# A fused attention layer on one core: values of two steps in one group, maxima of two heads in row halves, queries projected two slots ahead

## The reference

```python
qkv = einsum('bchw,oc->bohw', x, w_qkv);  q, k, v = split(qkv, 3)
q = q.reshape(b, 8, 64, n) * 64 ** -0.5          # k, v alike, unscaled
attn = softmax(einsum('bhdi,bhdj->bhij', q, k), axis=-1)
out = einsum('bhij,bhdj->bhid', attn, v)
y = einsum('bchw,oc->bohw', out, w_out) + b_out
y = y * rsqrt(mean(y * y, axis=1) + 64 ** -0.5) * rms_scale
return y + x
```

## Time and profile before

| | before |
|---|---|
| median of 3 runs | 4428.12 us (4426.63 to 4432.22) |
| the profiled execution's span | 4424.5 us |
| PE busy | 4317.8 us, 98% |
| DVE busy | 2982.6 us, 67% |
| POOL busy | 2722.1 us, 62% |
| ACT busy | 1984.7 us, 45% |

### The profile page before, as it was taken

One profiled execution on the slowest core, in us unless ns is written; L12 is line 12 of the kernel. 1 busy time (PEld: TensorE's weight loads), 2 busy tenths in 40 slices (PEclk: granted clock), 3 DMA queues, 4 the chain that ended last, 5 costly groups with the idle time before them and its releaser, 6 DMA issues.

```text
span 4424.5 us, 61545 instructions
## 1 busy us (share of the span) xinstructions
PE 4317.8 (98%) x18752; PEld 2583.7 (58%) x18752; DVE 2982.6 (67%) x2506; ACT 1984.7 (45%) x3265; POOL 2722.1 (62%) x2092
## 2 busy tenths in 40 slices
PE   7999999999999999999999999999999999999996
PEld 5556565565655656555565655656556565565653
DVE  5567666676766667676666666676667766676665
ACT  3445444444444444444444444544445444454443
POOL 5566656665566665666666565665656755666565
PEclk9999999999999999999999999999999999999998
DMA  3111111111111101111021110211101111111100
GB/s 134 39 48 48 39 42 55 49 48 39 58 39 49 60 27 63 39 53 58 20 77 36 42 58 21 76 39 39 58 31 66 39 39 58 49 48 39 45 32 29
DMA packets 71359, 213.19 MB, mean 48 GB/s; under 512 B 8152, under 2 KB 8280, under 8 KB 58208
## 3 DMA queue, kind: packets, MB, share of 16 engines
q1 hardware_dynamic: 71008, 208.80, 13.4%
HBM read 168.92 MB, written 39.85 MB: 47 GB/s over the span
## 4 chain that ended last, share of the span: by engine, by line
PE 94%; DVE 3%; issue 2%; ACT 1%; POOL 0%; DMA 0%; POOLq 0%; SPq 0%; ACTq 0%; DVEq 0%
PE pv L539 22%; PE aux L424 16%; PE aux L477 12%; PE score L524 12%; PE score L526 10%; PE aux L460 8%; PE aux L505 8%; PE aux L491 2%; DVE maxima L749 2%; PE aux L484 1%; PE aux L514 1%; DVE x_lo L266 0%; ACT v_sb L623 0%; ACT x_hi L669 0%; DVE o_norm L794 0%
## 5 line engine op out<-in xcount | busy, mean ns | idle before, releaser
L884 POOL TENSOR_TENSOR prob_sum<-prob_sum,probs 128x512 f32<-128x512 f32 x1536 | 2004.4, 1333 | 538.0 <-ACT probs L593 537.4
L593 ACT ACTIVATE probs<-score 128x512 f32<-128x512 f32 x2048 | 1112.2, 595 | 1339.8 <-PE score L526 1264.4
L749 DVE TENSOR_REDUCE maxima<-aux 128x1 f32<-128x1024 f32 x1024 | 1236.9, 1218 | 300.1 <-PE aux L477 284.8
L539 PE MATMUL pv<-probs,v_sb 128*64 128x512 f32 x4096 | 1104.4, 618 | 0.0
L880 POOL TENSOR_TENSOR prob_sum<-probs 128x512 f32<-128x512 f32 x256 | 323.3, 1284 | 1062.8 <-ACT probs L593 1062.8
L524 PE MATMUL score<-q_hl,k_hh 128*128 128x512 f32 x2048 | 857.4, 419 | 24.1 <-ACT v_sb L623 22.8
L526 PE MATMUL score<-q_hm,k_l 72*128 72x512 f32 x2048 | 813.1, 397 | 0.0
L477 PE MATMUL aux<-k_hh,q_hl 128*128 128x512 f32 x2048 | 709.4, 428 | 22.3 <-DVE maxima L749 21.4
L424 PE MATMUL aux<-x_hi,w_ring 128*128 128x512 f32 x2048 | 646.1, 397 | 17.3 <-POOL x_lo L266 17.3
L477 PEld LDWEIGHTS aux<-k_hh,q_hl 128*128 128x128 f32 x2048 | 343.8, 189 | 489.0 <-issue 313.2
L524 PEld LDWEIGHTS score<-q_hl,k_hh 128*128 128x128 f32 x2048 | 386.5, 189 | 350.3 <-issue 205.5
(11 more groups left out here) (58 smaller groups left out, 3694.3 us busy)
## 6 DMA issues: line engine op xcount, KB each, us to landing
w_ring<-w_split SPq DMA_DIRECT2D x93, 1024.0 KB, 4.8
x_stage<-x SPq DMA_DIRECT2D x128, 256.0 KB, 4.4
resid<-x SPq DMA_DIRECT2D x128, 256.0 KB, 5.7
out<-resid SPq DMA_DIRECT2D x128, 256.0 KB, 2.0
w_split<-w_ring SPq DMA_DIRECT2D x3, 1024.0 KB, 12.1
w_split<-y_sb SPq DMA_DIRECT2D x3, 1024.0 KB, 3.8
y_sb<-wqkv SPq DMA_DIRECT2D x4, 512.0 KB, 8.3
probs<-wqkv SPq DMA_DIRECT2D x2, 512.0 KB, 7.0
```

Of the source, the lines that this page charges most:

```text
L539: pe.matmul(pv[half][e * D:(e + 1) * D, :], v_sb[:, pair // 2, j, (pair % 2) * P + e * D:(pair % 2) * P + (e + 1) * D], probs[:, j % 4, e, ...
L593: act.activation(probs[:, j % 4, e, :], score[e][:], ACT.Exp, scale=SOFT).then_inc(prob_ready, 1)
L749: dve.tensor_reduce(maxima[:, n:n + 1], aux[at][:], AX_X, ALU.max).then_inc(aux_free[at], 1)
L884: pool.tensor_tensor(prob_sum[:, e, :], prob_sum[:, e, :], probs[:, j % 4, e, :], ALU.add).then_inc(prob_added, 1)
```

## The change

A slot still has 8 steps, now laid out on 16 places of another order:

- The values of two steps are one group: places 1, 5, 9 and 13 hold the values of steps 2g-2 and 2g-1 (g = t // 4; at place 1 the last slot's steps 6 and 7). L stands at place 5, ahead of the values.
- Behind each value group stand the maxima of one query tile for both heads (`maxima_of_tile`). They use the queries' and keys' high parts alone, 64 rows each: head 0 in rows 0 to 63, head 1 in rows 64 to 127. For this, head 1's queries are kept with the high part in the upper rows. Each tile takes all four banks: head 0 banks 0 and 1, head 1 banks 2 and 3.
- The other items stand at places 3, 7, 11 and 15. K is two items of one bank, the values' projection four. T stands in the middle of Q at place 15, and is now one pass of a 128 x 128 product in the split form's operand type.
- Q projects for the slot after the next (`SLOT_QUERIES = 2`).
- `aux` is one tensor of four banks with their own counters.
- L's sums are copied to SBUF by ACT, and DVE inverts them in two halves at places 5 and 6; `normalise` moves to place 8, O0 and O1 to place 11.
- DVE splits five of x's eight parts in slot 6, POOL three. SP's weight loads wait for other items.

```diff
-SUMS_AT = (1, 1, 1, 1, 1, 1, 1, 1)
-VALUES_AT = (3, 3)
-MAXIMA_AT = [(4, 5, 6, 7, 8, 9, 10, 11)] * SLOTS
-OUTPUT_AT = [(12, 14)] * SLOTS
-NORMALISE_AT = 5
+SLOTS, STEPS, BLOCKS = 8, 8, 4
+PLACES = 4 * BLOCKS
+SLOT_QUERIES = 2
+SQUARE_AT = (2, 4, 6, 8)
+NORMALISE_AT = 8
+INVERT_AT = ((0, 12), (1, 12))
+ROOT_AT = ((1, 0), (2, 0))
+SCALE_AT = ((1, 2), (2, 2))
+REPEAT_AT = 10
+SPLIT_AT = (0, 1, 2, 4, 5, 6, 8, 9)
+SPLIT_BY_GPSIMD = (1, 3, 5)
...
+    if t % 4 == 1:
+        if t == 5 and preceding:
+            out.append(("L", 3))
+        if following:
+            out += [(f"M{t // 4}0", 0), (f"M{t // 4}1", 2)]
+    if t in (3, 7):
+        if slot in (0, 2, 4):
+            out.append((f"K{t // 4}", 0))
+        elif slot in (1, 3):
+            out.append((f"V{slot - 1 + t // 4}", 0))
+        elif slot == 7 and following:
+            out.append((f"V{t // 4}", 0))
+    if t == 11:
+        if preceding:
+            out += [("O0", 0), ("O1", 2)]
+        if slot == 6 and projected:
+            out.append(("K0", 0))
+        if slot == 7 and following:
+            out.append(("V2", 0))
+        if slot in (0, 1) and not first:
+            out.append(("R", 0))
+    if t == 15:
+        if following:
+            out.append(("T", 2))
+        if projected:
+            out.append(("Q", 0))
+        if slot == 6 and projected:
+            out.append(("K1", 1))
+        if slot == 7 and following:
+            out.append(("V3", 1))
...
+            def maxima_of_tile(body, slot, it):
+                nslot = (slot + 1) % SLOTS
+                npair, nhalf = divmod(nslot, 2)
+                ks = [claim(body, slot, f"M{it}{e}", two=True) for e in range(2)]
+                for h in range(2):
+                    for e in range(2):
+                        rows = slice(e * D, (e + 1) * D)
+                        last = pe.matmul(bank(ks[e] + h), q_hl[rows, nhalf, e, it * P:(it + 1) * P],
+                                         k_hh[rows, npair % 2, e, h * HALF:(h + 1) * HALF],
+                                         start=True, stop=True)
+                        if h == 1:
+                            last.then_inc(aux_full[ks[e]], 1)
...
-                    for t in range(HALF_STEPS):
-                        j = t // 2
+                    pe.wait_ge(q_repeated, 2 * (body.b * SLOTS + slot + 1))
+                    for t in range(PLACES):
+                        g = t // 4
+                        names = [name for name, _ in items_at(slot, t, body.first, body.last)]
                         if t % 2 == 0:
-                            scores(body, slot, j)
-                        elif j > 0:
-                            values(body, slot, j - 1, False)
+                            scores(body, slot, t // 2)
+                        elif t % 4 == 1:
+                            if "L" in names:
+                                item(body, slot, "L")
+                            for j in (2 * g - 2, 2 * g - 1):
+                                if g > 0:
+                                    values(body, slot, j, False)
+                                elif slot > 0:
+                                    values(body, slot - 1, STEPS + j, False)
+                                elif not body.first:
+                                    values(body, SLOTS - 1, STEPS + j, True)
+                            if f"M{g}0" in names:
+                                maxima_of_tile(body, slot, g)
+                        elif "Q" in names:
+                            item(body, slot, "Q", range(0, 2))
+                            item(body, slot, "T")
+                            item(body, slot, "Q", range(2, KT))
+                            for name in names:
+                                if name not in ("Q", "T"):
+                                    item(body, slot, name)
...
+                elif name == "L":
+                    done = body.b * SLOTS + slot
+                    k = body.full(act, slot, name)
+                    if not (body.first and slot == 1):
+                        act.wait_ge(onorm_ready, done - 1)
+                    act.activation(inv_sum[:], bank(k), ACT.Copy).then_inc(aux_free[k], 1)
...
+            def invert_sums(body, slot, part):
+                if part == 0:
+                    body.consumed(dve, slot, "L")
+                cols = slice(part * HALF // 2, (part + 1) * HALF // 2)
+                dve.reciprocal(inv_sum[:, cols], inv_sum[:, cols]).then_inc(inv_ready, 1)
...
+                        if t in (5, 6) and preceding:
+                            invert_sums(body, slot, t - 5)
+                        for name, _ in items_at(slot, t, body.first, body.last):
                             item(body, slot, name)
...
-                        if t == NORMALISE_AT and not (body.first and slot == 0):
+                        if t == NORMALISE_AT and preceding:
                             normalise(body, slot)
-                        if t == NORMALISE_AT + 2 and slot not in LOW_BY_GPSIMD:
+                        if t == NORMALISE_AT + 1 and slot not in LOW_BY_GPSIMD:
                             split_output_low(dve, body.b * SLOTS + slot)
```

More of the change, by code:

```diff
@@ L60, in items_at @@
     preceding = not (first and slot == 0)
     out = []
-    if t == 0 and following:
-        out.append("Q")
-    if t == SUMS_AT[slot] and preceding:
-        out.append("L")
-    if following:
-        out += [f"M{i}" for i, at in enumerate(MAXIMA_AT[slot]) if t == at]
-        if slot == 7:
-            out += {2: ["K"], 3: ["V0"], 15: ["V1"]}.get(t, [])
-    if slot in (1, 2) and t == VALUES_AT[slot - 1]:
-        out.append(f"V{slot - 1}")
-    if slot in (0, 1) and t == MEAN_AT[slot] and not first:
-        out.append("R")
@@ L99, in body_keys @@
-def body_keys(first, last):
-    return [(s, n) for s in range(SLOTS) for t in range(HALF_STEPS) for n in items_at(s, t, first, last)]
+    if t % 4 == 1:
[10 more added lines that the diff above has]
+            out.append((f"V{t // 4}", 0))
@@ L103, in attention_kernel, with body_items @@
+def body_items(first, last):
+    return [(s, n, k) for s in range(SLOTS) for t in range(PLACES) for n, k in items_at(s, t, first, last)]
 def attention_kernel(nc, x, wqkv, wout, bias, scale, consts, out):
@@ L486, in item @@
+                    last.then_inc(aux_full[k], 1)
+                elif name == "T":
+                    k = claim(body, slot, name)
+                    body.consumed(pe, slot, "M30")
+                    body.consumed(pe, slot, "M31")
+                    if body.plan is pro:
+                        pe.wait_ge(mask_set, 2)
+                    pe.matmul(bank(k)[:, 0:P], maxima[:], neg_ident[:],
+                              start=True, stop=True).then_inc(aux_full[k], 1)
                 elif name == "L":
@@ L694, in _ @@
             start = Body(pro, -1, True, True)
+            for slot, name, _ in PRO_ITEMS:
+                item(start, slot, name)
+                if (slot, name) == (6, "Q"):
+                    repeat_queries(start, 7)
             act.wait_ge(const_loaded, 64)
-            for name in PRO_ITEMS:
-                item(start, 7, name)
             act.wait_ge(w_set, 3)
@@ L741, in item @@
[L741 to L745 removed]
+                        ins = dve.tensor_tensor(k_l1[0:D, kp, e, cols], bank(k)[rows[e], :],
+                                                k_hh[rows[e], kp, e, cols].bitcast(F32), ALU.subtract)
+                    ins.then_inc(aux_free[k], 1)
+                    for e in range(2):
+                        dve.tensor_copy(k_hh[rows[1 - e], kp, e, cols], k_hh[rows[e], kp, e, cols].bitcast(F32))
@@ L820, in one @@
                 for slot in range(SLOTS):
-                    for t in range(HALF_STEPS):
+                    preceding = not (body.first and slot == 0)
+                    for t in range(PLACES):
                         if (slot, t) in SCALE_AT and not body.first:
@@ L849, in _ @@
             dve.tensor_copy(tile_mask[:], raw_mask).then_inc(mask_set, 1)
-            dve.wait_ge(mask_set, 1)
+            dve.tensor_copy(neg_ident[:], raw_ident).then_inc(mask_set, 1)
+            dve.wait_ge(mask_set, 2)
             start = Body(pro, -1, True, True)
-            for name in PRO_ITEMS:
-                item(start, 7, name)
+            for slot, name, _ in PRO_ITEMS:
+                item(start, slot, name)
             run_bodies(dve, one)
             end = Body(epi, B, False, True)
-            item(end, 0, "L")
+            for part in range(2):
+                invert_sums(end, 0, part)
             normalise(end, 0)
```

405 lines of the change are left out of this document (180 added, 225 removed).

## The result

The changed kernel takes 5013.17 us (median of 4 runs, 5006.92 to 5017.71) against 4427.38 before: 1.132 times the time, 95% interval 1.1304 to 1.1336. I had forecast 4484 and a range up to 4625. The sign was right, the size wrong by 529 us: the change cost ten times what I had forecast.

What follows compares the result with a forecast made beforehand. Bound by PE's instruction stream; PE saves 20.8 us a batch (268.2 to 247.4), waits add 27.3; with slot schedules, 275.2 against 271.9, plus prologue and epilogue: 4484 us, 1.3% slower. Own range 4425 to 4545; eight in ten 4290 to 4625.

Steps and rivals of the forecast that it cites:

- The value group: Values of two steps in one group on PE: 2.01 us where 2.45 stood; four groups save 1.75 a slot.
- the maxima in pairs: Maxima groups on PE, two pairs in row halves: 0.76 us each; four groups 3.0 a slot for 3.7.
- T: T in one pass on PE, at place 15: saves 0.15 us a slot.
- Rival 2: Maxima groups: row halves don't run side by side, 7.9 us a batch more, 4610 us; chance 0.12.
- rival 3: Maxima groups: weights of a row half wait for that half's matmul, 0.11 us a group, 4540 us; chance 0.05.
- the waits in the batch: PE's added waits on DVE, the output projection's chain and late reductions: 15.0 + 8.7 + 2.4 + 1.2 = 27.3 us a batch.
- `o_lo` from DVE in slots 2 and 6: Before O0 at place 11, behind group 2's reductions in program order: 2.5 us more in slot 2, 4.0 in slot 6.
- Rival 1: Places 7 and 11: DVE's chain isn't late, only 0.43 us bank waits remain, 4306 us; chance 0.30 in full, 0.12 by half.
- Batch 247.4 + 27.3: One batch: 247.4 us if nothing waited plus 27.3 of waits, 274.7 against 271.9 before.
- PE busy near 90%: Sign in the trace after: PE busy near 90% of the span, against 98% before, would bear the forecast out.
- two subtractions and two copies, 2.1: K1's work on DVE in slot 4, in the chain to the output projection: 2.1 us.
- POOL's work stays off the path: GpSimd's work, unchanged in number, 21 us a slot in at least 27, stays off the path.

Runs made afterwards that it cites:

- a_filler: Changed kernel plus eight useless matmuls on TensorE ahead of O0's wait for `o_lo` in slots 0, 1, 2 and 6: 4928.27 us.
- a_korder: Changed kernel with VectorE making the keys' second copy ahead of their low part, maxima still in row halves: 4859.87 us.
- a_sums_early: Changed kernel with L (TensorE's sums and ScalarE's copy of them) at place 1 instead of 5: 5174.06 us.
- a_hint_kcopies: Changed kernel with a prefetch hint for the loop's closing branch and the keys' second copy on ScalarE instead of VectorE: 4751.46 us.

## Why the prediction was wrong

**Right: what PE saves, by its steps.** The value group (1.87 for 1.91), the maxima in pairs (0.67 to the next score and 0.10 more inside it, for 0.76), T (0.06 to the next matmul, for 0.17). Rival 2, row halves that don't overlap, and rival 3, their weights waiting, are refuted by the earlier trace rows against the group above. What these savings are worth to the kernel is another matter: pairing alone gained nothing, row halves 44 us.

**Near, in part by luck: the waits in the batch.** I summed 27.3 us a batch. The waits that the trace lists for PE in the batch from 2553.05 to 2863.6 are 36.2, and 6.2 of them are the loop's top: 30.0 where I had 27.3. That the sums lie so close is luck in part: in slots 3 and 7 PE waits 0.7 us each where I had 1.9, at place 7 of slots 0, 2 and 4 it waits 2.6 where I had 1.0, 1.6 and 0.5, and for `o_lo` in slot 1 3.8 where I had 0.4. `o_lo` from DVE in slots 2 and 6: forecast waits 2.9 and 4.4, measured 3.16 and 4.12. Rival 1 is refuted: DVE's chain is late. PE's idle time in the whole run is 647 us (5004.8 - 4358.2), where I had announced 400.

**Wrong, the largest: the sum took all of PE's work at 2.4 GHz.** I read the clock of the kernel before and carried it over to a kernel whose waits I had just raised to 27 us a batch. Its place in the prediction is the line "Batch 247.4 + 27.3". For the batch from 2553.05 to 2863.6 it should have read: 247.4 of work as I had it, 36.2 of waits, 3.4 for the weight load of 0.1 us behind each of the 34 waits (the listing doesn't count it as idle), and the clock. The granted clock was 1.2 GHz in 47.8 us of that batch; PE waited in 10.2 of them, and of the other 37.6 half is lost, 18.8. That makes 306 of 310.5. In the batch of before, from 1975.07 to 2246.99, no time was at 1.2 GHz, and 268.2 + 3.1 gives 271.3 of 271.9. The 18.8 is an estimate from the clock's rows. a_filler shows that the term exists, 85 us of it by filling four places. The next two points are in part the same microseconds, since their waits bring the clock down. And my sign "PE busy near 90%" came out, with 87%, beside a forecast that failed: a matmul at 1.2 GHz is listed as busy for longer, 0.63 us for 0.39.

**Wrong: the loop's closing branch wasn't in the sum.** The prediction went from batch to batch as if code were straight. It cost 148 us here and 30 before. The row that would have told me was in the trace of before, with another name on it (waits):

```profile
PE score L524 <- ACT v_sb L623: 22.8, 13, 2.0
```

PE's scores waited 13 times for ACT's copy of V, once for each branch back. And SP's loads, which I had costed at nothing, are worth 35 us at this place.

**Wrong: K's copies at 0.35 us each.** "two subtractions and two copies, 2.1" was 4.3 for K0 of slot 0 (1.39 + 2.93), and such copies stand in four slots of eight. They are ahead of group 1's reductions on DVE, and PE waits for those at place 7 (slot 0, DVE and PE):

```profile
2527.85 2.36 DVE L760 TENSOR_REDUCE maxima<-aux 128x1 fp32r<-128x1024 f32 x2
```

```profile
2529.13 0.73 PE L422 MATMUL aux<-x_hi,w_ring 128*128 128x512 f32 x2 [2.63 <-DVE maxima L760]
```

My sum had 0.43 and 0.6 there. With another order of the copies PE's waits for reductions fell from 200.1 to 86.4 us (a_korder), and the order alone is worth 153 us. I had halved a duration of the earlier trace rows, and that was wrong twice: it was taken at place 15, where POOL was idle in 127 of 128 cases, and even with POOL idle half the columns take 422 ns, not 348.

**Wrong: "POOL's work stays off the path".** I counted its work, not when it may start. POOL may overwrite `prob_sum` only after L is read; L moved from place 1 to 5, so POOL begins late in the slot and then has a queue. In slot 1 ACT had `o_hi` ready at 2574.66:

```profile
2574.03 0.63 ACT L658 ACTIVATE o_hi<-o_norm 128x512 fp32r<-128x512 f32 x1
```

and POOL, in its own order, was at work on two residual parts and had two more sums to do:

```profile
2571.56 1.29 POOL L905 TENSOR_TENSOR prob_sum<-prob_sum,probs 128x512 f32<-128x512 f32 x1
2572.81 2.96 POOL L911 TENSOR_TENSOR resid<-resid,y_sb 128x512 f32<-128x512 f32 x2
2575.73 2.49 POOL L905 TENSOR_TENSOR prob_sum<-prob_sum,probs 128x512 f32<-128x512 f32 x2
2578.18 1.71 POOL L277 TENSOR_TENSOR o_lo<-o_norm,o_hi 128x512 fp32r<-128x512 f32 x1
```

`o_lo` starts at 2578.18 and O0 waits 3.79 us where I had 0.43. The price of this alone isn't settled, since a_sums_early moved POOL and DVE against each other.

**What stays open.** By experiment, 262 us of the 529 missed are the branch and the copies, with what they drag along. The remaining 267 were not divided by experiment. By the trace of a_hint_kcopies they are 16.5 us a batch (291.7 where I had 275.2). Of a batch 22.1 us are at 1.2 GHz, and PE waits in 6.8 of them, which leaves about 7.6 for the clock; its waits, 27.7, are with the weight loads behind them about 3.5 more than my 27.3; some 5 have no row that I can name. What POOL's queue costs within this stays open.

## What to carry to other kernels

When a change adds waits to a PE-bound kernel, price them twice: once as idle time, and once as the matmuls behind them at half clock, 0.43 us for 0.23. When a consumer is moved later, ask who is waiting to overwrite what it reads (here POOL behind L). Take an SBUF-to-SBUF duration of DVE only from a moment when POOL does what it will do then. A loop whose body is long should have its closing branch prefetched; that was worth 0.7% to the kernel before and 3% to the one after.

## What the runs showed of the hardware

- In the changed kernel the granted clock was 1.2 GHz for some microseconds behind waits of 2.6 to 5 us, and PE's matmuls were 0.43 apart there. It fell behind shorter waits too: behind 20 of 23 waits of about 1.7 us that PE had entered at full clock. In a_filler matmuls kept 0.23 behind a wait of 1.48 us, with eight useless matmuls ahead of it.
- A closing branch cost PE 1.8 us in one kernel, and 1.8 and 5.0 us in two pieces in another; the hint took all of it away.
- One float32 copy of 64 x 512 from SBUF to SBUF on DVE took 419 to 425 ns with POOL idle and 1367 on average beside POOL's work (93 and 143 copies of the changed kernel); one scaling of 128 x 512 took 747 (122 of them) and 1749 (4). Subtractions with an operand in PSUM took 686 and 687, and the row maxima, read from PSUM, 1219 and 1217.
- Two 64-row matmuls of 512 columns in the two row halves run side by side: four, in two pairs, took 0.67 us to the start of the next score, whose first matmul took 0.33 and not 0.23.
